# First loads reordered over two queues, a narrower wait for the scan, and the first keys moved ahead of the first norm

## What is computed

```python
x = _layernorm(x + _L0_attn_ref(x, A, B, W, b))            # u = x B^T ; h[t] = A*h[t-1] + u[t] ; y = h W^T + b
x = _layernorm(x + _L0_xattn_ref(x, ctx, ctx, Wq, bq, ...)) # q from x, k and v from ctx; RoPE; window of 50; 16 heads
x = _layernorm(x + _L0_ffn_ref(x, router_w1, router_w2, w1, w2, w3))  # 16 experts, each picks its top 64 tokens
```

## Time and profile before

| | us |
|---|---|
| median of 3 runs | 1119.21 (1119.19 to 1119.34) |
| the profiled execution's own time | 1119.52 |
| its span, first to last instruction | 1117.7 |
| TensorE busy in the span | 1010.7 (90%) |
| VectorE / GpSimd / ScalarE busy | 729.1 / 691.3 / 586.4 |

### The profile page before, as it was taken

How to read it: one execution, slowest core, us unless ns; L and a number is a source line. 1 busy time by engine, 2 the same in 40 slices (tenths; PEclk the granted TensorE clock), 3 DMA queues, 4 the chain that set the end, 5 groups by cost and what they waited for, 6 DMA issues and landing times.

```text
span 1117.7 us, 21898 instructions
## 1 busy us (share of the span) xinstructions
PE 1010.7 (90%) x6436; PEld 850.4 (76%) x6436; DVE 729.1 (65%) x2174; ACT 586.4 (52%) x1226; POOL 691.3 (62%) x785
## 2 busy tenths in 40 slices
PE   4789999999999998876999999999999999999990
PEld 3577777777777776644888788888888888888890
DVE  4577777777777777753577746556565664756534
ACT  1155555455555556434565556556565556656541
POOL 4456666566666666225476677777767676777644
PEclk8799999999999999966999999999999999999996
DMA  5333333333333332324566656666577665666646
GB/s 169 87 99 91 101 96 96 97 95 97 96 96 95 96 78 70 112 77 140 181 162 131 170 113 171 136 154 158 131 203 177 157 156 134 170 123 169 142 95 178
DMA packets 108848, 142.44 MB, mean 127 GB/s; under 512 B 15184, under 2 KB 75856, under 8 KB 108624
## 3 DMA queue, kind: packets, MB, share of 16 engines
q1 hardware_dynamic: 81728, 106.88, 32.6%
q0 software_dynamic: 24576, 33.57, 17.5%
q10 hardware_dynamic: 2448, 0.91, 0.4%
HBM read 90.71 MB, written 29.36 MB: 107 GB/s over the span
## 4 chain that ended last, share of the span: by engine, by line
PE 49%; DMA 2%; DVE 1%; ACT 1%; POOL 1%; issue 1%; SPq 0%; DVEq 0%; POOLq 0%; ACTq 0%
PE gate_bank L1247 15%; PE y_bank L1247 15%; PE value_bank L1247 15%; PE turn_bank L1257 2%; DMA acc_rows<-y,slots_now 1%; DMA last<-acc_rows 0%; DMA rw<-in_rw 0%; DVE stats L1423 0%; PE y_bank L1300 0%; DVE w_lo L1398 0%; DVE last L1434 0%; POOL acc_rows L1207 0%; POOL rw_placed L1226 0%; ACT w_hi L1324 0%; ACT gate L1337 0%
## 5 line engine op out<-in xcount | busy, mean ns | idle before, releaser
L1207 POOL DMA_INDIRECT acc_rows<-y,slots_now x128 | 202.6, 1583 | 127.9 <-ACT y L1351 99.3
L1416 DVE TENSOR_TENSOR hidden<-gate,value_bank 128x512 f32<-128x512 f32 x128 | 87.9, 687 | 194.8 <-ACT gate L1337 189.3
L746 ACT ACTIVATE probsT<-scoreT 128x356 f32<-128x356 f32 x256 | 117.8, 470 | 165.9 <-PE scoreT L593 84.7
L893 DVE CUSTOM_DVE_ANT_0 scored<-score,band 128x178 f32<-128x178 f32 x512 | 149.9, 337 | 83.3 <-PE score L564 76.6
L1337 ACT ACTIVATE gate<-gate_bank 128x512 f32<-128x512 f32 x128 | 76.6, 599 | 158.0 <-PE value_bank L1247 158.0
L1247 PE MATMUL y_bank<-w_hi,h_hi 128*128 128x256 f32 x512 | 146.9, 287 | 2.8 <-DVE weight_of L153 2.7
L1247 PE MATMUL y_bank<-w_lo,h_hi 128*128 128x256 f32 x512 | 142.6, 279 | 0.0
L1247 PE MATMUL y_bank<-w_hi,h_lo 128*128 128x256 f32 x512 | 142.6, 278 | 0.0
L1398 DVE TENSOR_TENSOR w_lo<-arena,w_hi 128x1024 fp32r<-128x1024 f32 x96 | 117.6, 1226 | 25.9 <-ACT w_hi L1324 25.9
L564 PE MATMUL score<-k_stack,q_stack 96*128 96x178 f32 x512 | 124.4, 326 | 8.2 <-DVE nmax L893 5.3
L564 PEld LDWEIGHTS score<-k_stack,q_stack 96*128 96x128 f32 x512 | 88.8, 192 | 36.5 <-DVE nmax L893 19.6
(11 more groups left out here) (177 smaller groups left out, 2415.0 us busy)
## 6 DMA issues: line engine op xcount, KB each, us to landing
arena<-in_w SPq DMA_DIRECT2D x96, 512.0 KB, 4.0
k_stack<-high_k SPq DMA_DIRECT2D x128, 64.0 KB, 2.3
q_stack<-high_q SPq DMA_DIRECT2D x128, 64.0 KB, 2.3
arena<-in_x SPq DMA_DIRECT2D x16, 256.0 KB, 2.9
arena<-in_xT SPq DMA_DIRECT2D x16, 256.0 KB, 3.2
arena<-in_cT SPq DMA_DIRECT2D x16, 256.0 KB, 3.5
k_stack<-low_k SPq DMA_DIRECT2D x64, 64.0 KB, 2.3
q_stack<-low_q SPq DMA_DIRECT2D x64, 64.0 KB, 2.3
```

The lines of the kernel that those rows point to most:

```text
L746: nc.scalar.activation(probsT[g % 2][:, u % HG, :, :].rearrange("p a s -> p (a s)"), scoreT[u % 2][:, 0:2 * SPAN], ACT.Exp, scale=1.0 / DH ...
L893: op = nc.vector.tensor_tensor_reduce(scored[t % 2][:, q, :], score[t % 2][:, q * SPAN:(q + 1) * SPAN], band[:, q, :], -1.0, BIG, ALU.add, ...
L1207: nc.gpsimd.indirect_dma_start(dram["acc"][c], bass.IndirectOffsetOnAxis(ap=now[:, m:m + 1], axis=0), y[m][:], None, compute_op=ALU.add).t ...
L1416: nc.vector.tensor_tensor(hidden[f % 2][:], gate[f % 2][:], value_bank[f % 2][:], ALU.mult).then_inc(hidden_ready, 1)
```

## The change

The first loads are issued in another order: SP's queue now begins with xT, xin, cT, wk, ww, and wb is issued by ScalarE behind acol. `halves` counts on the semaphore `bv`, so that `columns` needs 48 and the waiters of `bv` need 48; a wait of ScalarE for `bv` is added in step 0 where `halves` is first read. The keys of batch 0 move from step -1 to step -2: on TensorE behind U at t = 6 (ahead of Y), on ScalarE the bias at t = 7 and the high part at t = 12, on VectorE shuffle and product at t = 7 (ahead of the statistics of Y), on GpSimd cosine and rotation ahead of the refinement of Y's deviation and the subtraction for the low part behind it.

```diff
--- before.py
+++ after.py
@@ -318,6 +318,11 @@
 
             return (t - lag) // HG
 
+        FIRST_KEYS = Iter(0, -1, 4)
+
+        def hoisted(it):
+            return it.fixed and it.i == -1
+
         def has(it, n):
 
             return it.batch(0) if n >= 0 else it.batch(-1)
@@ -325,17 +330,16 @@
         @block.sync
         def _(sp):
             def load_x(par, b):
+                sp.dma_start(xT[par][:], dram["xT"][b].rearrange("(k p) s -> p k s", p=P)).then_inc(x_in[par], 16)
                 sp.dma_start(xin[par][:], dram["x"][b].rearrange("(t p) d -> p t d", p=P)).then_inc(x_in[par], 16)
-                sp.dma_start(xT[par][:], dram["xT"][b].rearrange("(k p) s -> p k s", p=P)).then_inc(x_in[par], 16)
 
             def load_c(par, b):
                 sp.dma_start(cT[par][:], dram["cT"][b].rearrange("(k p) s -> p k s", p=P)).then_inc(c_in[par], 16)
 
-            sp.dma_start(wb[:], weight("mix_BT")).then_inc(const_in["wb"], 16)
             load_x(0, 0)
-            sp.dma_start(ww[:], weight("mix_WT")).then_inc(const_in["ww"], 16)
             load_c(0, 0)
             sp.dma_start(wk[:], weight("WkT")).then_inc(const_in["wk"], 16)
+            sp.dma_start(ww[:], weight("mix_WT")).then_inc(const_in["ww"], 16)
             sp.dma_start(cos[:], dram["cos"]).then_inc(const_in["rope"], 16)
             sp.dma_start(sin[:], dram["sin"]).then_inc(const_in["rope"], 16)
             sp.dma_start(wq[:], weight("WqT")).then_inc(const_in["wq"], 16)
@@ -477,7 +481,7 @@
 
                 pool.wait_ge(ready["X"], uses(it, "X", 1))
                 if not it.at_least(1):
-                    pool.wait_ge(const_in["bv"], 32)
+                    pool.wait_ge(const_in["bv"], 48)
                 x = x1[it.r % 4]
                 nc.gpsimd.tensor_tensor(x[:], x[:], bo[:].unsqueeze(1).to_broadcast([P, TT, D]),
                                         ALU.add).then_inc(x1_biased, 1)
@@ -496,15 +500,19 @@
                         pool.wait_ge(x1_ready, it.lin(1, 2))
                     nc.gpsimd.tensor_tensor(xb[:], xin[par][:], b_mix[:].unsqueeze(1).to_broadcast([P, TT, D]),
                                             ALU.add).then_inc(xb_ready, 1)
+                if it.fixed and it.i == -2:
+                    pool.wait_ge(const_in["rope"], 32)
+                    cosine(FIRST_KEYS, 0)
+                    rotate(FIRST_KEYS, 0)
                 if there(it, "K"):
-                    if not it.at_least(0):
-                        pool.wait_ge(const_in["rope"], 32)
-                    cosine(it, 0)
-                    rotate(it, 0)
+                    if not hoisted(it):
+                        cosine(it, 0)
+                        rotate(it, 0)
                     cosine(it, 1)
                 if there(it, "Q"):
                     rotate(it, 1)
-                    lower(it, 0)
+                    if not hoisted(it):
+                        lower(it, 0)
                     lower(it, 1)
                 if behind:
                     inverse_sums(it, -2)
@@ -512,6 +520,8 @@
                     inverse_deviation(it, "O")
                 if there(it, "Y"):
                     inverse_deviation(it, "Y")
+                if it.fixed and it.i == -2:
+                    lower(FIRST_KEYS, 0)
                 if behind:
                     inverse_sums(it, -1)
 
@@ -632,8 +642,13 @@
                         mm = nc.tensor.transpose(out[:, k * S + n * P:k * S + (n + 1) * P], x[:, n, k * P:(k + 1) * P], ident[:])
                 mm.then_inc(ready[name], 1)
 
+            def keys(it):
+
+                first_use(it, "K", "wk")
+                pe.wait_ge(c_in[(it.r + 1) % 2], it.pairs(16, 1))
+                project(it, "K", wk, cT[(it.r + 1) % 2])
+
             def step(it):
-                fill = it.fixed and it.i == -1
                 for t in range(NH):
                     heads(it, t)
                     if t in (1, 5, 9, 13):
@@ -641,10 +656,10 @@
                     turned_heads(it, t)
                     if t in (2, 6, 10, 14):
                         gather(it, t)
-                    if t == (0 if fill else 1) and there(it, "K"):
-                        first_use(it, "K", "wk")
-                        pe.wait_ge(c_in[(it.r + 1) % 2], it.pairs(16, 1))
-                        project(it, "K", wk, cT[(it.r + 1) % 2])
+                    if t == 1 and there(it, "K") and not hoisted(it):
+                        keys(it)
+                    if t == 6 and it.fixed and it.i == -2:
+                        keys(FIRST_KEYS)
                     if it.fixed and it.i == NB - 1 and t == 1:
                         pe.wait_ge(rw2_set, 1)
                         pe.wait_ge(silu_done, 1)
@@ -719,6 +734,7 @@
         @block.scalar
         def _(act):
             act.dma_start(acol[:], dram["mix_A"]).then_inc(const_in["columns"], 16)
+            act.dma_start(wb[:], weight("mix_BT")).then_inc(const_in["wb"], 16)
             act.dma_start(bq[:], dram["bq"]).then_inc(const_in["columns"], 16)
             act.dma_start(bk[:], dram["bk"]).then_inc(const_in["columns"], 16)
             act.dma_start(b_mix[:], dram["mix_b"].partition_broadcast(P)).then_inc(const_in["b_mix"], 16)
@@ -726,8 +742,8 @@
             act.dma_start(band[:], dram["band"].rearrange("(t p) k -> p t k", p=P)).then_inc(const_in["band"], 16)
             act.dma_start(bv[:], dram["bv"].partition_broadcast(P)).then_inc(const_in["bv"], 16)
             act.dma_start(bo[:], dram["bo"].partition_broadcast(P)).then_inc(const_in["bv"], 16)
-            act.dma_start(halves[:], dram["halves"]).then_inc(const_in["columns"], 16)
-            act.wait_ge(const_in["columns"], 64)
+            act.dma_start(halves[:], dram["halves"]).then_inc(const_in["bv"], 16)
+            act.wait_ge(const_in["columns"], 48)
 
             act.sem_inc(x2_kept, 1)
             for name, n in FREED_EARLY.items():
@@ -772,6 +788,8 @@
                     if counts(it.lin(NPAIR, g // 2 - 1)):
                         act.wait_ge(attnT_ready, it.lin(NPAIR, g // 2 - 1))
                     b = g // 2 % 2
+                    if it.fixed and it.i == 0:
+                        act.wait_ge(const_in["bv"], 48)
                     nc.scalar.activation(vals[b][:], attn[0][:, 0:S], ACT.Copy, scale=halves[:, 0:1])
                     nc.scalar.activation(mixed[b][:], attn[0][:, 0:S], ACT.Copy, scale=halves[:, 1:2]).then_inc(even_kept, 1)
 
@@ -814,13 +832,14 @@
                 nc.scalar.copy(out[:].rearrange("p k s -> p (k s)"), bank(name)[:]).then_inc(freed[name], 1)
 
             def step(it):
-                fill = it.fixed and it.i == -1
                 for t in range(NH):
                     if t in (1, 5, 9, 13):
                         keep_maxima(it, t)
                     exponentials(it, t)
-                    if t == (1 if fill else 2) and there(it, "K"):
+                    if t == 2 and there(it, "K") and not hoisted(it):
                         biased(it, 0)
+                    if it.fixed and it.i == -2 and t == 7:
+                        biased(FIRST_KEYS, 0)
                     if t == 1 and there(it, "X"):
                         columns(it, "X", x1T)
                     if t in (7, 15):
@@ -829,8 +848,10 @@
                         invert_sums(it, (t - 20) // 8)
                     if t == 4 and there(it, "Q"):
                         biased(it, 1)
-                    if t == 5 and there(it, "K"):
+                    if t == 5 and there(it, "K") and not hoisted(it):
                         heighten(it, 0)
+                    if it.fixed and it.i == -2 and t == 12:
+                        heighten(FIRST_KEYS, 0)
                     if t == 9 and there(it, "O"):
                         estimate(it, "O")
                     if t == 7 and there(it, "Q"):
@@ -869,7 +890,7 @@
             for n in range(NG):
 
                 nc.vector.memset(nmax[n][:], 0.0).then_inc(fixed_set, 1)
-            dve.wait_ge(const_in["columns"], 64)
+            dve.wait_ge(const_in["columns"], 48)
 
             def met():
 
@@ -946,8 +967,10 @@
                         dve.wait_ge(odd_added, it.lin(NPAIR, p + 1))
                         met()
                         nc.vector.stream_shuffle(sums[b][:], mixed[b][:], swap).then_inc(sums_ready, 1)
-                    if t == 3 and there(it, "K"):
+                    if t == 3 and there(it, "K") and not hoisted(it):
                         rotated(it, 0)
+                    if it.fixed and it.i == -2 and t == 7:
+                        rotated(FIRST_KEYS, 0)
                     if t == 5 and there(it, "Q"):
                         rotated(it, 1)
                     if t == 8 and there(it, "O"):
@@ -978,7 +1001,7 @@
                         if it.at_least(1):
                             dve.wait_ge(attn_ready, it.lin(NG, 0))
                         if not it.at_least(0):
-                            dve.wait_ge(const_in["bv"], 32)
```

(1 more changed line is left out.)

## The result

The changed kernel takes 1113.05 us (median of four runs, 1111.58 to 1114.97) against 1119.20 for the kernel before on the same chip (1118.86 to 1119.34). The medians lie 6.15 us apart. The ratio of the two kernels' runs is 0.995 with an interval of 0.9932 to 0.9969, which is 5.6 us less (3.5 to 7.6). The forecast was 2.5 us, and its range ended at 1114.7, a gain of 4.5. The profiled execution is the slowest of the four: 1114.97, of which 1113.1 is span.

A forecast was written before the change was run, and what follows sets the result against it. TensorE, busy 90% of the span, bounds the kernel; an earlier start shifts everything. 2.66 (pre_Y earlier) - 0.92 (slower normalisation) + 0.8 (clock) = 2.5 us, so 1119.2 - 2.5 = 1116.7; range 1114.7 to 1119.5.

The forecast's parts named there:

- The path: First two batches: each step from scan to X(1) waits for the one before, so this chain is to be shortened.
- Part 1, the scan's wait: Start of batch 0: scan follows U without waiting for halves; alone, Y moves from 15.54 to about 12.6, gaining 2.9 us.
- Part 2, the loads: First transfers reordered: U starts at about 5, K at 10.2 once wk lands, sin's table in time.
- Rivals 2 and 4: Early loads no faster: 1117.6, chance 0.15; and wk late, so K ahead of Y delays the chain: 1121.8, chance 0.05.
- Part 3, the hoist: K of batch 0 ahead of Y: pre_Y at 16.75, 2.66 us earlier; normalisation slowed by 0.92; x1(0) 1.74 earlier.
- Part 4, the clock: Projections up to X(1): three could gain the full clock, one lose it; +0.8 us, bounds -1.8 and +1.8.
- rival 1: Q or U(1) of the first two batches, or K(1), at full clock: gain 3.6 or more, 1115.6, chance 0.10.
- Part 4, the one-to-one hand-over: From x1(0) on: its 1.74 us reach the hand-over to the pipeline, and all later times shift by one amount.

The follow-up runs named there:

- experiments 2 and 8: Changed kernel with batch 0's K back behind Y: 1114.02 (0.9952), repeated 1113.77 (0.9926); also with ww third on SP's queue: 0.9938 and 0.9933.
- experiment 1: Kernel before with only halves moved to the semaphore of bv, so the scan no longer waits for it: 1114.5 us, ratio 0.996.
- experiment 3: Kernel before with the hoist alone: 1119.57 us, ratio 1.0003; kernel before with the new order of loads alone: 1122.04 us, ratio 1.0014.
- experiment 4: Changed kernel with GpSimd's subtraction for low_k of batch 0 one step later, behind x1(0): 1115.62 us, ratio 0.9954.
- the variants of before: Kernel before with one, two or eight added ScalarE waits that are met at once: ratios 0.9984, 0.9992 and 0.9988.
- filling: Unread matmuls in TensorE's gaps: 24 calls in the changed kernel, 1125.36 us (1.0035); 26 calls in the changed kernel without the hoist, 1121.26 us (1.0006).

## Why the prediction was wrong, by its own steps

**The path: right.** Scan, Y, x1(0), X, Q, U(1), Y(1), x1(1), X(1) is the chain. Kernels that brought x1(0) further forward (experiments 2 and 8) also started X(1) earlier. The first score came at 38.31 (about 38 was foretold) and TensorE then waited for x1(1).

**Part 1, the scan's wait: right.** The scan was released by U. Taken alone the text gave the edit 2.9 us at Y, from the U of the earlier trace rows; in experiment 1 Y was 1.6 earlier behind a U that started 1.0 later, 2.6 in all. In time it brought 4.5 us (2.8 to 6.0), more than its step; its one profile shows the same two terms as the whole change: X(1) 3.3 earlier for 1.6 at x1(0), which goes with the clock, and a loop shorter by 1.1.

**Part 2, the loads: right.** U started at 5.48 (about 5), K at 10.57 (10.2), held by wk, and `sin` was there in time. Rivals 2 and 4 didn't occur. In experiment 3 the order alone was worth nothing, as rival 2 would have it, but because `halves` still held the scan.

**Part 3, the hoist: sizes right, its sign not asked.** pre_Y began at 16.86 (16.75), released by VectorE's product, Y rose to the full clock, and the normalisation took 1.65 (1.65); experiment 4 gives the 0.92 back. x1(0) came 1.63 earlier (1.74). But the text compared each step only with before, never with the change without the hoist. Experiments 2 and 8 do: x1(0) at 19.63 and 19.38 without it, at 22.42, 22.02 and 21.36 with it. On the two chips where both ran, the hoist costs 1.5 us (0.9952 against 0.9965, intervals that overlap) and 2.8 us (0.9926 against 0.9951, intervals that only touch).

**Part 4, the clock: right in the mean, wide for one run.** +0.8 was taken with bounds of 1.8 either way. The profiled pair gave 1.8 at X(1) and 2.6 at the 100th matmul, which is rival 1's picture (gain 3.6 or more, 1115.6), with U(1) at the full clock. Over all profiles it is 0.9 at X(1), or 0.6 with the variants of before. Rival 1's price is thus a price of one run. The term is as large as was said, but that is in part luck. The reason given was a count (three projections that could gain, one that could lose) and a shorter idle stretch; in the runs the low stretches fell differently in each execution of one and the same kernel, and its spread at X(1), 2.7 us over four profiles of the changed kernel, is three times the term. Of the three projections that could gain only U(1) ever ran at the full clock without filling: it took 3.52 us or more in all three profiles of before and in one of the four after.

**Part 4, the one-to-one hand-over: the step that failed.** "From there on all times should be shifted by one amount." The shift grew in the loop, by 1.46 us in the profiled pair and by 1.51 in the means. The sum had no term for it. The text looked for a loop that takes the gain back and not for one that adds to it, and it gave the two instructions that the change adds to ScalarE, the issue of wb and the wait for `bv`, no price at all. With it the sum up to the end of the loop is 2.1 at x1(0), 0.9 of clock and 1.5 in the loop, 4.5 us. The four comparisons of the changed kernel (0.995, 0.9965, 0.9951, 0.9976) have a mean of 0.9961, 4.4 us. They agree more closely than the runs allow, since behind the loop the profiles differ by more than that (the low stretch near 635, and the stretch in the next paragraph). Of the 2.0 us by which the forecast of 2.5 was short of this, 1.5 are the loop and most of the rest is x1(0), 2.1 in place of 1.74. The 5.6 of the first comparison lies another 1.1 above, inside its interval of 3.5 to 7.6. The mean of 4.4 would still have been in the range, whose end was a gain of 4.5; that the first comparison fell outside it is in part the draw of its runs.

**What stays open.** By what mechanism added instructions on ScalarE shorten the loop, and whether their number counts. Why the loads alone, whose loop was 0.8 shorter, gained nothing in time. And the spread between runs of one kernel, 3 to 10 us on the chips of the experiments: the stretch from the 3790th to the 6340th matmul, in the expert stage, took 433.4 to 434.9 us in some profiles and 436.7 to 437.6 in others. The four profiles of the changed kernel all had the shorter stretch, two of three of before the longer; of the variants close to the changed kernel, low_k later had the longer, and of the two profiles without the hoist one had the longer and one the shorter. No edit touches that stretch, and whether the changed kernel meets the shorter one more often isn't settled.

## What to carry to other kernels

Look first for a semaphore shared by several loads: the wait that narrows it cost a few lines here and by itself measured as much as the whole change, and the loads' order moved x1(0) only together with it. Before moving work ahead of the critical step because its engine is idle there, compare with the change without that move, and not only with the kernel before; here the idle time had vanished with the first edit, so that the moved work stood in the way. Where the clock or a loop may differ by a microsecond or two, profile each kernel three times, and split the shift at marks (before the loop, behind it) before a cause is named.

## What the runs showed of the hardware that was not expected

- Some 50 more matmul instructions ahead of the loop, each with its weight load, lengthened the loop from 385.7 to 394.1 us: 3 us stalls with no releaser, each with an instruction fetch that begins with it, low stretches of the clock behind them, and 54 packets on the instruction queue in place of 35.
- One to four more instructions ahead of the loop on ScalarE, waits that are met at once, shortened the loop of 387.3 us (mean of before) by 0.7 to 2.1 us, in one profile for each of three kernels.
- One program on the same data had its first low stretches in different places, which moved X(1) between 38.9 and 41.6 us after, and between 42.2 and 44.1 before.
- A float32 matmul call is two instructions in the trace (24 added calls, 48 more instructions), so the eight of a projection, 1.97 us at the full clock and 3.75 at the lower, are four calls.
